# Inverting the 16x16 diagonal blocks of a delta-rule layer off TensorE: one block per partition on VectorE and GpSimd, carried through DRAM

## The chip, the cores and the metric

The kernel runs on one core of one Trainium2 chip. The metric is device time in microseconds (us) of one execution, the median of several. Before the change it is 2876.7 us, the median of three runs (2873.14, 2876.70 and 2880.99).

## What is computed

Two transformer layers on 4 sequences of 512 tokens with 256 features. Layer 0 adds to its input a gated delta-rule attention (32 value heads, 16 key heads, 128 features each) and a mixture of 64 experts; layer 1 adds a small attention and a mixture of 8 experts. The change touches the delta rule alone. The reference runs it token by token:

```python
def step(Sm, inp):
    q_, k_, v_, g_, b_ = inp
    Sm = Sm * jnp.exp(g_)[..., None, None]
    kv = jnp.einsum('bhk,bhkv->bhv', k_, Sm)
    delta = (v_ - kv) * b_[..., None]
    Sm = Sm + jnp.einsum('bhk,bhv->bhkv', k_, delta)
    o = jnp.einsum('bhk,bhkv->bhv', q_, Sm)
    return (Sm, o)
```

The kernel runs it in chunks of 128 tokens. Within a chunk the tokens depend on each other through a unit triangular 128x128 matrix, whose inverse is needed for every batch element and value head.

## The kernel before, in words

The program has three parts. The first (L65) normalizes the tokens, makes the gates and the routing. The second (`heads_and_experts`, L437) is the long one: 64 steps, one for each pair of key head and chunk (`STEPS`), each with 8 triangular matrices (2 value heads x 4 sequences). The third (L1774) gathers the experts' results and computes layer 1.

A step is written out by hand as a fixed order of calls for each engine, and three steps overlap: in step g the engines project and convolve step g's tokens, invert the matrices of step g-1, and use the inverses of step g-2. TensorE's order is in `step` at L945, ScalarE's (ACT) at L1236, VectorE's (DVE) at L1541, GpSimd's (POOL) at L1705 and that of the load queue (SP) at L690. Every engine works its list strictly in order, and semaphores join the lists; a call that waits holds everything behind it on its engine.

The matrix of step g is made by DVE in `decayed_products` (L1420, four multiplications of PSUM by the decays, tile `ATP`). ACT's `compact` (L1134) copies the 32x32 diagonal blocks into `ATc` (128 partitions x 256). These are inverted by doubling. `first_level` (L1430, DVE) makes the 2x2 inverses with a mask, a subtraction from the identity and a transpose. Then come four levels (1 to 4). Each is: 32 small products on TensorE (`level_x`, L789, two instruction records each), a copy on ACT (`inverse_copy`, L1151), 32 more products (`level_y`, L803), and on DVE `level` (L1441): a subtraction of PSUM and a 32x32 transpose. GpSimd makes the levels' masked operands in two calls of `mask` (L1639). Level 1 of a step begins late in that step, levels 2, 3 and 4 follow in the next. Levels 5 and 6 then join the 32x32 blocks to 64 and to 128.

Other calls that the text speaks of: `project` (L731) and `project_z` (L745), the projections of the tokens; `evacuate` (L1091, ACT), which copies a projection out of PSUM; `conv` (L1374, DVE), three multiply-adds for each of four channel groups, both tensor operands in SBUF; `squares` (L1119, ACT); `row_scales` (L1491, DVE), which waits for `out_squares` (L1200) and for `squares` of the queries, and runs a chain of small dependent operations (L50 to L58); `gather_out`, `residual`, `level6`, `outputs`, `new_state` and `rows_decay` on DVE; `scaled_decays`, `rho_w`, `gated`, `state_decay` and `normed` on GpSimd. In the first 8 steps GpSimd also issues 16 indirect DMAs per step (`scatter`, L1695). TensorE's `slot_free` (L714) makes a product wait until the PSUM bank that it reuses has been read: `project(g, 3)` waits there for the last of `decayed_products`, and the expert's gate product (`EX_GATE`, L939) for `squares` of the queries.

On SP each step loads, in this order, the decays of the step (`decays_in`, into the single tile `ab`), the step's expert (`unit_in`) and, for some steps, weights (`head_in`).

Of the kernel before, what the change touches and what calls it, by code (L numbers as in the profile page):

```python
# [5 lines left out]
F32 = mybir.dt.float32  # L6
# [58 lines left out]
def layernorm_and_gates(nc, A, R, adram, xnbuf, xbuf, routes):  # L65
# [7 lines left out]
    with ExitStack() as ctx:  # L73
# [59 lines left out]
        zero_set, zeroed = sem("zero_set"), sem("zeroed")  # L133
        head_loaded, head_high = sem("head_loaded"), sem("head_high")
        dve_step, pool_step = sem("dve_step"), sem("pool_step")
# [5 lines left out]
        def _(sp_):  # L141
# [8 lines left out]
            for dst, src in ((R["w_raw"][:, :, :], A["w_in"][0, :, :].rearrange("p (k n) -> p k n", k=KT)), (R["cw_raw"][:, :, :], A["conv_w"][0, :, :].rearrange("p (k n) -> p k n", k=4)),  # L150
                             (R["normw"][:, :], A["norm_w"]), (R["masks"][:, :, :], A["masks"]), (R["identc"][:, :], A["identc"])):
                sp_.dma_start(dst, src).then_inc(head_loaded, 16)
            sp_.wait_ge(zero_set, 1)
            for q in range(NE // 4):
                sp_.dma_start(xbuf[EARLY * CAP + q * 512:EARLY * CAP + (q + 1) * 512, :].rearrange("(p r) d -> p (r d)", p=P), zero[:, :]).then_inc(zeroed, 16)
# [9 lines left out]
            sp_.wait_ge(stored, 16 * (B + 3))  # L165
            sp_.wait_ge(zeroed, 16 * NE // 4)
# [89 lines left out]
        def _(dve):  # L256
# [36 lines left out]
            dve.wait_ge(head_loaded, 80)  # L293
# [68 lines left out]
            dve.tensor_tensor(put_u[:, :, :].bitcast(I32), slot_u[:, :, :].bitcast(I32), over_i[:, :, :], ALU.bitwise_or)  # L362

        @block.gpsimd
        def _(pool):
# [6 lines left out]
            pool.memset(zero[:, :], 0.0).then_inc(zero_set, 1)  # L372
# [19 lines left out]
            pool.memset(aT[:, :, :, 0:1], 0.0).then_inc(aT_copied, 1)  # L392

# [12 lines left out]
    inverse_mm=(("x2", 1), ("x6", 2), ("y6", 2), ("y2", 1), ("x3", 1), ("y3", 1), ("x4", 1), ("y4", 1), ("x5", 1), ("x1", 0), ("y1", 0), ("y5", 1)),  # L406
    inverse_sb=((6, 2), (2, 1), (3, 1), (4, 1), (1, 0), (5, 1)),
    inverse_d=((2, 1), (3, 1), (4, 1), (1, 0), (5, 1)),
# [5 lines left out]
LEVELS = 5  # L414
BLK = 32
PARTS = [(kt, wp, xp) for kt in range(KT) for wp, xp in ((0, 0), (0, 1), (1, 0))]
# [5 lines left out]
           compact=4, masked=2, halved=2, spread=4, t5=3, tt=1,  # L422
# [14 lines left out]
def heads_and_experts(nc, A, R, adram, xnbuf, xbuf, ybuf):  # L437
# [22 lines left out]
    with ExitStack() as ctx:  # L460
        sb = lambda n, s, d=F32: ctx.enter_context(nc.sbuf_tensor("p2_" + n, s, d))
        sem = lambda n: ctx.enter_context(nc.semaphore("p2_" + n))
        w_raw, w_hl, cw_raw, cw, masks, identc, normw = (R[n] for n in ("w_raw", "w_hl", "cw_raw", "cw", "masks", "identc", "normw"))
# [21 lines left out]
        M = sb("M", [P, LEVELS - 1, 2, B, BLK])  # L485
# [35 lines left out]
        dstep, init = sem("dstep"), sem("init")  # L521
# [77 lines left out]
        def vb(ap, n=BLK):  # L599
            return ap.rearrange("p (g t) -> p g t", t=n)  # L600

# [42 lines left out]
        def _(sp):  # L644
# [44 lines left out]

            def step(g):  # L690
                decays_in(g)
                unit_in(g)
                head_in(g)
# [3 lines left out]
            for j in range(TAIL):  # L697
                x_, gu_, d_ = tail_buffers(j)
# [14 lines left out]
        def _(pe):  # L713
# [75 lines left out]
            def level_x(g, l):  # L789
# [3 lines left out]
                wait(pe, "masked", g, 1 if l < 3 else 2)  # L793
                if l == 1:
                    wait(pe, "tt", g - 2, 1)
                pe.nop(nofuse=True)
                for n in range(2 * B):
                    v, b = n // B, n % B
                    for q in range(4):
                        m = pe.matmul(psI[p][quad(q), n * BLK:(n + 1) * BLK], M[quad(q), l - 1, v, b, :], Dc[p][quad(q), v, b, :], start=True, stop=True)  # L800
# [144 lines left out]
            def step(g):  # L945
                project(g, 0)
                if g >= 1:
                    level_x(g - 1, 2)
# [8 lines left out]
                if g >= 1:  # L957
                    level_y(g - 1, 2)
                if g >= 2:
# [5 lines left out]
                if g >= 1:  # L965
                    level_x(g - 1, 3)
                if g >= 2:
                    within(g - 2, 0)
                if g >= 1:
                    turn_values(g - 1, 0)  # L970
                    level_y(g - 1, 3)
# [24 lines left out]
                level_x(g, 1)  # L996
# [6 lines left out]
                level_y(g, 1)  # L1003
# [36 lines left out]
            level_x(STEPS - 1, 2)  # L1040
# [4 lines left out]
            level_y(STEPS - 1, 2)  # L1045
# [3 lines left out]
            level_x(STEPS - 1, 3)  # L1049
# [3 lines left out]
            level_y(STEPS - 1, 3)  # L1053
# [36 lines left out]
        def _(act):  # L1090
# [43 lines left out]
            def compact(g):  # L1134

                wait(act, "atp", g, 4)
                wait(act, "masked", g - 1, 2)
                wait_event(act, "inverse_d", 1, g - 1)
                for q in range(4):
                    act.activation(heads(ATc[quad(q), :, :, :]), heads(ATP[g % 2][quad(q), :, :, 0, quad(q)]), ACT.Copy).then_inc(s["compact"], 1)  # L1140
# [95 lines left out]
            def step(g):  # L1236
# [9 lines left out]
                if g >= 1:  # L1246
                    inverse_copy(g - 1, 2)
                if g >= 2:
# [11 lines left out]
                if g >= 1:  # L1260
                    inverse_copy(g - 1, 3)
                if g >= 2:
# [14 lines left out]
                compact(g)  # L1277
# [6 lines left out]
                inverse_copy(g, 1)  # L1284
# [34 lines left out]
            inverse_copy(STEPS - 1, 2)  # L1319
# [4 lines left out]
            inverse_copy(STEPS - 1, 3)  # L1324
# [36 lines left out]
        def _(dve):  # L1361
            count = [0]
# [67 lines left out]
            def first_level(g):  # L1430
# [972 lines left out]
```

## Time and profile before

| | |
|---|---|
| median of three runs | 2876.7 us |
| span of the profiled execution, first to last instruction | 2973.8 us |
| TensorE (PE) busy | 2684.9 us, 90% of the span |
| VectorE (DVE) busy | 2384.7 us, 80% |
| ScalarE (ACT) busy | 1828.3 us, 61% |
| GpSimd (POOL) busy | 1221.2 us, 41% |
| mean granted TensorE clock | 0.954 |

Times in the profile are microseconds unless marked ns. The profiled execution's own time is its span of 2973.8 us; no time beyond the span is listed for it, and it is 97.1 us longer than the median of the timed runs. In the page's slices of the span, PE is at nine tenths or more from about 300 us to 2500 us: the 64 steps. What lies before is the first part and the filling of the steps, what lies behind is their draining and layer 1. [...]

### The profile page before, as it was taken

The numbers are of one execution on the slowest core, as the hardware profiler recorded it, in microseconds if no ns is written. First come the engines' busy times: TensorE is split into PE (matmuls) and PEld (weight loads), VectorE is DVE, ScalarE is ACT, GpSimd is POOL, SyncE is SP. The second block draws the span as 40 slices with busy tenths as digits, with TensorE's granted clock in tenths as the row PEclk, the third lists the DMA queues.
The fourth block names the chain that finished last, engine by engine and source line by source line (L and its number), as shares of the span: only waits on it lengthen the run. The fifth ranks groups of instructions, "written<-read, shape, count | busy, mean of one in ns | idle before, by whom it ended". The sixth has DMA issues, their size and how long they took to land. (4 is left out here: it accounts for less than half of the span.)

```text
span 2973.8 us, 122804 instructions
## 1 busy us (share of the span) xinstructions
PE 2684.9 (90%) x52271; PEld 2275.1 (77%) x52272; DVE 2384.7 (80%) x5006; ACT 1828.3 (61%) x5749; POOL 1221.2 (41%) x1048
## 2 busy tenths in 40 slices
PE   1478889999999999999999999999999999857898
PEld 1367668888888888888888888888888888724555
DVE  7556658888888888888888888888888888468796
ACT  1245546777777777777777777777777777501111
POOL 2456555343434343434343434343434343255420
PEclk7778889999999999999999999999999999978999
DMA  5221101111111111111111111111111110152311
GB/s 189 92 61 42 32 23 38 35 42 35 42 35 42 35 42 35 42 36 41 39 42 41 39 39 42 41 40 37 42 35 42 35 32 28 61 192 90 94 64 43
DMA packets 92834, 153.27 MB, mean 52 GB/s; under 512 B 16966, under 2 KB 60661, under 8 KB 91107
## 3 DMA queue, kind: packets, MB, share of 16 engines
q1 hardware_dynamic: 69491, 111.65, 12.9%
q0 software_dynamic: 12288, 24.19, 2.6%
q10 hardware_dynamic: 10512, 9.57, 0.9%
q8 instruction: 415, 6.80, 0.9%
q14 instruction: 128, 1.05, 0.1%
HBM read 114.38 MB, written 40.37 MB: 52 GB/s over the span
## 5 line engine op out<-in xcount | busy, mean ns | idle before, releaser
L1383 DVE SCALAR_TENSOR_TENSOR p_y<-p_xr,cw,p_y 128x512 f32<-128x512 f32 x768 | 652.2, 851 | 66.7 <-ACT p_y L1101 46.6
L740 PE MATMUL p_psF<-xnS,w_hl 128*128 128x512 f32 x1536 | 432.8, 417 | 24.1 <-PEq L628 11.1
L1655 POOL TENSOR_TENSOR p_Wr<-p_Ws,p_rho 128x512 f32<-128x512 f32 x96 | 135.8, 1436 | 651.0 <-ACT p_Ws L1198 651.0
L740 PEld LDWEIGHTS p_psF<-xnS,w_hl 128*128 128x128 f32 x1536 | 279.3, 195 | 87.3 <-issue 18.2
L1637 POOL TENSOR_TENSOR p_E<-p_E,p_sj 128x512 f32<-128x512 f32 x128 | 158.0, 1253 | 292.9 <-DVE p_sj L1409 292.9
L800 PEld LDWEIGHTS p_psI<-p_Dc,p_M 32*32 32x32 f32 x16384 | 180.1, 106 | 100.0 <-issue 91.9
L922 PE MATMUL p_psO<-p_wout,p_ont 128*128 128x256 f32 x1024 | 250.4, 399 | 0.7 <-ACT p_ont L1211 0.7
L800 PE MATMUL p_psI<-p_Dc,p_M 32*32 32x32 f32 x16384 | 215.7, 195 | 38.1 <-issue 33.7
L1678 POOL TENSOR_TENSOR p_O<-p_OG,p_sm 128x512 f32<-128x512 f32 x128 | 131.4, 1049 | 240.9 <-DVE p_sm L58 240.8
L1098 ACT ACTIVATE p_xr<-p_psF 128x512 f32<-128x512 f32 x256 | 154.1, 602 | 123.0 <-PE p_psF L740 119.8
L810 PEld LDWEIGHTS p_psI<-p_Xs,p_DTc 32*32 32x32 f32 x16384 | 168.5, 106 | 75.0 <-issue 70.0
L810 PE MATMUL p_psI<-p_Xs,p_DTc 32*32 32x32 f32 x16384 | 199.3, 195 | 27.0 <-ACT p_Xs L1158 14.3
L922 PEld LDWEIGHTS p_psO<-p_wout,p_ont 128*128 128x128 f32 x1024 | 197.7, 198 | 30.2 <-ACT p_ont L1211 1.1
L1204 ACT ACTIVATE p_O<-p_OG 128x128 f32<-128x128 f32 x512 | 152.0, 298 | 111.4 <-POOL p_OG L1672 109.4
L755 PE MATMUL p_psF<-w_hl,xnS 128*128 128x256 f32 x1536 | 214.5, 290 | 5.0 <-issue 1.7
L755 PEld LDWEIGHTS p_psF<-w_hl,xnS 128*128 128x128 f32 x1536 | 198.8, 193 | 16.0 <-ACT p_y L1101 4.6
L1158 ACT ACTIVATE p_Xs<-p_psI 128x256 f32<-128x256 f32 x320 | 124.1, 388 | 126.0 <-PE p_psI L800 85.1
L1445 DVE TENSOR_TENSOR p_Dc<-p_Dc,p_psI 128x256 f32<-128x256 f32 x256 | 104.4, 408 | 97.6 <-PE p_psI L810 97.0
L1644 POOL TENSOR_TENSOR p_M<-p_ATc,masks 128x512 f32<-128x512 f32 x128 | 175.2, 1369 | 8.7 <-ACT p_ATc L1140 8.6
L1101 ACT ACTIVATE p_y<-p_psF,cw 128x512 f32<-128x512 f32 x256 | 176.8, 691 | 1.6
L1418 DVE TENSOR_TENSOR_SCAN p_E<-p_ab,p_identr 128x512 f32<-128x512 f32 x128 | 171.2, 1338 | 6.9 <-DMA p_ab<-decays 6.9
L1427 DVE TENSOR_TENSOR p_ATP<-p_psF,p_E 128x512 f32<-128x512 f32 x256 | 158.8, 681 | 22.4 <-PE p_psF L786 17.7
(322 smaller groups left out, 6638.8 us busy)
## 6 DMA issues: line engine op xcount, KB each, us to landing
p_ab<-decays SPq DMA_DIRECT2D x64, 512.0 KB
w_raw<-in_w_in SPq DMA_DIRECT2D x16, 768.0 KB, 5.6
p_wgu<-in_w_gu SPq DMA_DIRECT2D x60, 176.0 KB
expert_out<-p_ye ACTq DMA_DIRECT2D x73, 128.0 KB, 1.8
expert_in<-p_zero SPq DMA_DIRECT2D x16, 512.0 KB, 7.1
p_xe<-expert_in SPq DMA_DIRECT2D x60, 128.0 KB
p_wd<-in_w_down SPq DMA_DIRECT2D x60, 88.0 KB
p_wout<-in_w_out SPq DMA_DIRECT2D x16, 256.0 KB
```

The lines of the kernel that those rows point to most:

```text
L740: m = pe.matmul(b4(psF[f % 2][:, :]), w_hl[:, wp, kt, ty * P:(ty + 1) * P], xnS[:, xp, kt, :].rearrange("p (b t) -> p b t", b=B)[:, :, c * ...
L755: m = pe.matmul(psF[f % 2][:, (b % 2) * 2 * P:(b % 2 + 1) * 2 * P], xnS[:, xp, kt, b * S + c * P:b * S + (c + 1) * P], w_hl[:, wp, kt, 4 * ...
L800: m = pe.matmul(psI[p][quad(q), n * BLK:(n + 1) * BLK], M[quad(q), l - 1, v, b, :], Dc[p][quad(q), v, b, :], start=True, stop=True)
L810: m = pe.matmul(psI[p][quad(q), 256 + n * BLK:256 + (n + 1) * BLK], DTc[p][quad(q), v, b, :], Xs[p][quad(q), v, b, :], start=True, stop=True)
L922: m = pe.matmul(psOO[:, b * D:(b + 1) * D], ont[:, v, b, :], wout[:, v, :], start=(v == 0), stop=(v == 1))
L1098: act.activation(xr[:, ty, :, TAPS - 1:], b4(psF[f % 2][:, :]), ACT.Copy)
L1101: act.activation(y[:, ty, :, :], b4(psF[f % 2][:, :]), ACT.Copy, scale=cw[:, ty, TAPS - 1:TAPS]).then_inc(s["drained"], 1)
L1383: m = dve.scalar_tensor_tensor(y[:, ty, :, :], xr[:, ty, :, tap:tap + P], cw[:, ty, tap:tap + 1], y[:, ty, :, :], ALU.mult, ALU.add)
L1418: dve.tensor_tensor_scan(flat(E[:, v, :, :]), flat(ab[:, v, :, :]), flat(identr[:, :, :]), 0.0, ALU.mult, ALU.add).then_inc(s["scan"], 1)
L1427: dve.tensor_tensor(ATP[g % 2][:, v, two, :, :], psF[f % 2][:, :].rearrange("p (b u t) -> p b u t", b=2, u=2), E[:, v, two, :].unsqueeze(2 ...
L1637: pool.tensor_tensor(E[:, v, :, :], E[:, v, :, :], over(sj[:, :, v]), ALU.mult).then_inc(s["diag"], 1)
L1644: pool.tensor_tensor(M[:, two, :, :, :].rearrange("p l v b t -> p l (v b) t"), heads(ATc[:, :, :, :]).unsqueeze(1).to_broadcast([P, 2, 2 * ...
```

## The change

The 32x32 blocks are no longer built up from 2x2. Each holds two 16x16 blocks on its diagonal, 64 of them in a step; these are inverted one per partition, and only level 4 (16 to 32) stays on TensorE. Per step:

- ACT: `compact(g)` writes the negated blocks and moves forward in its list, ahead of `squares(g, 1)`. The copies of levels 1 to 3 are gone.
- SP: `cores_out(g)` stores `ATc` to a DRAM buffer, waits, and loads the 64 blocks into `U`, one per partition, by two DMAs of 512 runs of 64 bytes. `cores_back(g-1)` waits for the inverses, stores them by two such DMAs into a second DRAM buffer (whose other elements stay zero), waits, and loads that buffer into `DTc`. A step's order is now `cores_back(g-1)`, the loads of step g+1, `cores_out(g)`, the weights of step g+1.
- DVE: `pivots(g-1)` at the place of `level(g-1, 1)`: a memset of the diagonals, then for k = 1 to 6 a product and an addition on both 8x8 halves of 64 partitions (12 to 24 elements per partition), each waiting for the one before. `turn_cores(g-1)`, one 32x32 transpose, at the place of `level(g-1, 3)`; it waits for the load into `DTc`. `first_level` and levels 1, 2 and 3 are gone.
- GpSimd: `join(g-1)` at the head of its step: two 8x8 matrix products per partition, each a multiplication of 512 elements and additions of 256, 128 and 64, all in a chain. The two calls of `mask` become one of half the size.
- TensorE: `level_x` and `level_y` of levels 1, 2 and 3 are gone: 192 small products per step.

```diff
+            def cores_out(g):
+                wait(sp, "compact", g, 4)
+                sp.dma_start(block_rows(blocks_out), ATc[:, :, :, :].rearrange("p v b t -> p (v b t)")).then_inc(apart, 16)
+                sp.wait_ge(apart, 16 * (g + 1))
+                for s_ in range(2):
+                    at = slice(s_ * CORES // 2, (s_ + 1) * CORES // 2)
+                    sp.dma_start(U[at, 0:CORE * CORE], core_rows(blocks_out, s_)).then_inc(gathered, 16)
+
+            def cores_back(g):
...
+                wait(sp, "joined", g, 1)
+                for s_ in range(2):
+                    at = slice(s_ * CORES // 2, (s_ + 1) * CORES // 2)
+                    sp.dma_start(core_rows(blocks_back, s_), U[at, 0:CORE * CORE]).then_inc(returned, 16)
+                sp.wait_ge(returned, 16 + 32 * (g + 1))
+                wait(sp, "spread", g - 2, 4)
+                sp.dma_start(DTc[g % 2][:, :, :, :].rearrange("p v b t -> p (v b t)"), block_rows(blocks_back)).then_inc(inverted, 16)
...
             def step(g):
-                decays_in(g)
-                unit_in(g)
-                head_in(g)
+                cores_back(g - 1)
+                loads(g + 1)
+                cores_out(g)
+                if g + 1 < STEPS:
+                    head_in(g + 1)
...
-            def first_level(g):
+            def pivots(g):
+
+                dve.wait_ge(gathered, 32 * (g + 1))
+                mark(dve.memset(diagonal, 1.0))
+                for k in range(1, HALF_CORE - 1):
+                    n = HALF_CORE - 1 - k
+                    column = halves_of[:, :, 0:k, k:k + 1].to_broadcast([CORES, 2, k, n])
+                    row = halves_of[:, :, k:k + 1, k + 1:].to_broadcast([CORES, 2, k, n])
+                    rest, product = halves_of[:, :, 0:k, k + 1:], pivot[:, :, 0:k, 0:n]
+                    link(dve.tensor_tensor(product, column, row, ALU.mult))
+                    m = dve.tensor_tensor(rest, rest, product, ALU.add)
+                    if k < HALF_CORE - 2:
+                        link(m)
+                m.then_inc(s["pivoted"], 1)
+
+            def turn_cores(g):
 
                 p = g % 2
                 wait(dve, "halved", g - 2, 2)
-                wait(dve, "spread", g - 2, 4)
                 wait_event(dve, "inverse_mm", "x5", g - 2)
-                wait(dve, "compact", g, 4)
-                link(dve.tensor_tensor(heads(Dc[p][:, :, :, :]), heads(ATc[:, :, :, :]), masks[:, 0, :].unsqueeze(1).to_broadcast([P, 2 * B, BLK]), ALU.mult))
-                link(dve.tensor_tensor(heads(DTc[p][:, :, :, :]), identc[:, :].unsqueeze(1).to_broadcast([P, 2 * B, BLK]), heads(Dc[p][:, :, :, :]), ALU.subtract))
+                dve.wait_ge(inverted, 16 * (g + 1))
                 dve.transpose(heads(Dc[p][:, :, :, :]), heads(DTc[p][:, :, :, :])).then_inc(s["inverse_d"], 1)
...
+            def join(g):
+
+                n = [CORES, HALF_CORE, HALF_CORE, HALF_CORE]
+                lo, hi = slice(0, HALF_CORE), slice(HALF_CORE, CORE)
+                wait(pool, "pivoted", g, 1)
+                for half, left, right in ((0, square[:, lo, lo], square[:, lo, hi]), (1, halfway[:, :, :], square[:, hi, hi])):
+                    link(pool.tensor_tensor(terms[:, :, :, :], left.rearrange("p i k -> p k i").unsqueeze(3).to_broadcast(n), right.unsqueeze(2).to_broadcast(n), ALU.mult))
+                    for k in (4, 2):
+                        link(pool.tensor_tensor(terms[:, 0:k, :, :], terms[:, 0:k, :, :], terms[:, k:2 * k, :, :], ALU.add))
+                    if half == 0:
+                        link(pool.tensor_tensor(halfway[:, :, :], terms[:, 0, :, :], terms[:, 1, :, :], ALU.add))
+                    else:
+                        pool.tensor_tensor(square[:, lo, hi], terms[:, 0, :, :], terms[:, 1, :, :], ALU.add).then_inc(s["joined"], 1)
...
                 if g >= 2:
                     out_squares(g - 2, 0)
                     out_squares(g - 2, 1)
+                compact(g)
                 squares(g, 1)
                 if g >= 1:
                     inverse_copy(g - 1, 4)
                 evacuate(g, 3)
                 expert(g, EX_GATE)
-                compact(g)
```

## Rows read from the trace of the kernel before

**Rows 1.** Windows: busy us of each engine (x instructions), granted clock, DMA share, GB/s.
```profile
800.00:1600.00 800.00, 783.37 (x17483) 692.36 (x17482) 687.13 (x1358) 595.59 (x1913) 316.74 (x264) 1.00 0.15 39
282.00:340.00 58.00, 46.70 (x815) 38.85 (x812) 35.07 (x66) 27.19 (x88) 39.81 (x37) 0.82 0.13 43
```

**Rows 2.** One line's instructions: DVE's gather_out, once a step (ns min/median/max, first and last start).
```profile
L1514 DVE TENSOR_TENSOR acc<-acc,p_psO x43: 1181/1182/1184, 812.7 to 2356.7; 128x1024 f32<-128x1024 f32 x43
```

**Rows 3.** Timeline, TensorE, one step: start, us, what [idle before].
```profile
1530.65 0.60 PE L939 MATMUL p_psF<-p_xeT,p_wgu 128*88 128x128 f32 x4
...
1547.98 0.75 PE L800 MATMUL p_psI<-p_Dc,p_M 32*32 32x32 f32 x64
1548.67 1.14 PE L846 MATMUL p_psI<-p_D64X,p_ATP 64*64 64x64 f32 x16
```

**Rows 4.** Timeline, VectorE, the same step.
```profile
1525.49 2.48 DVE L1427 TENSOR_TENSOR p_ATP<-p_psF,p_E 128x512 f32<-128x512 f32 x4 [0.39 <-PE p_psF L786]
...
1530.36 0.17 DVE L1502 TENSOR_SCALAR p_xq<-p_ss 128x4 f32<-128x4 f32 x1 [0.46 <-ACT p_y L1126]
...
1534.52 0.74 DVE L1437 TENSOR_TENSOR p_Dc<-p_ATc,masks 128x256 f32<-128x256 f32 x1
1535.29 1.41 DVE L1438 TENSOR_TENSOR p_DTc<-identc,p_Dc 128x256 f32<-128x256 f32 x1
...
1537.89 3.58 DVE L1383 SCALAR_TENSOR_TENSOR p_y<-p_xr,cw,p_y 128x512 f32<-128x512 f32 x3
...
1545.95 0.42 DVE L1445 TENSOR_TENSOR p_Dc<-p_Dc,p_psI 128x256 f32<-128x256 f32 x1 [0.43 <-PE p_psI L810]
1546.41 0.45 DVE L1446 STREAM_TRANSPOSE p_DTc<-p_Dc 128x256 f32<-128x256 f32 x1
1546.78 1.18 DVE L1514 TENSOR_TENSOR acc<-acc,p_psO 128x1024 f32<-128x1024 f32 x1
...
1549.42 2.33 DVE L1383 SCALAR_TENSOR_TENSOR p_y<-p_xr,cw,p_y 128x512 f32<-128x512 f32 x3 [0.43 <-ACT p_y L1101]
...
1553.84 0.68 DVE L1450 TENSOR_SCALAR p_TT<-p_psI 64x512 f32<-64x512 f32 x1 [1.05 <-PE p_psI L855]
...
1560.73 0.42 DVE L1445 TENSOR_TENSOR p_Dc<-p_Dc,p_psI 128x256 f32<-128x256 f32 x1 [0.44 <-PE p_psI L810]
...
1562.90 2.48 DVE L1427 TENSOR_TENSOR p_ATP<-p_psF,p_E 128x512 f32<-128x512 f32 x4 [0.39 <-PE p_psF L786]
```

**Rows 5.** Groups by line, 800 to 2400 us: busy us, mean ns | idle before.
```profile
L56 DVE TENSOR_TENSOR p_sm<-p_sm 128x12 f32<-128x12 f32 x129 | 22.1, 171 | 4.4
```

**Rows 6.** Timeline, ACT, the same step: the four copies of compact.
```profile
1531.61 1.72 ACT L1140 ACTIVATE p_ATc<-p_ATP 32x256 f32<-32x256 f32 x4
```

**Rows 7.** Timeline, GpSimd: first part, then the same step.
```profile
61.33 2.17 POOL L385 TENSOR_TENSOR p_sp<-p_sp,p_pl 128x512 f32<-128x512 f32 x1 [11.96 <-DVE p_pl L320]
...
1538.88 1.26 POOL L1644 TENSOR_TENSOR p_M<-p_ATc,masks 128x512 f32<-128x512 f32 x1
```

**Rows 8.** One line's instructions: GpSimd's smallest product, 800 to 2400 us.
```profile
L1686 POOL TENSOR_TENSOR p_hb<-p_gsb,p_usb x44: 451/682/909, 804.1 to 2389.2; 88x128 f32<-88x128 f32 x44
```

**Rows 9.** DMA issues: count, KB each, median us from issue to landing.
```profile
expert_out<-p_ye ACTq DMA_DIRECT2D x73, 128.0 KB, 1.8
...
p_wbc<-expert_weights SPq DMA_DIRECT2D x4, 512.0 KB, 5.1
```

**Rows 10.** Timeline, the load queue, the same step.
```profile
1559.37 0.39 SPq L648 DMA_DIRECT2D p_ab<-decays  x1
```

**Rows 11.** Timeline, TensorE: a wait ahead of a half-speed stretch.
```profile
469.68 0.60 PE L821 MATMUL p_psI<-p_Dc,p_ATP 32*32 32x32 f32 x27 [1.22 <-DVE p_DTc L1446]
```

**Rows 12.** Windows around it: columns as in rows 1.
```profile
460.00:471.20 11.20, 8.70 (x200) 6.67 (x199) 10.58 (x25) 5.31 (x11) 8.71 (x9) 1.00 0.03 6
471.20:474.60 3.40, 3.40 (x9) 2.78 (x9) 3.36 (x5) 3.13 (x8) 2.27 (x2) 0.50 0.00 0
```

More of the change, by code:

```diff
@@ L164, in _ @@
             sp_.dma_start(routes[:, 2 * NT * NE:], kept[:, 2 * NT * NE:]).then_inc(stored, 16)
-            sp_.wait_ge(stored, 16 * (B + 3))
-            sp_.wait_ge(zeroed, 16 * NE // 4)
+            sp_.wait_ge(stored, 16 * (B + 3 + NE // 4))
         @block.tensor
@@ L370, in link @@
                 ch.wait()
-            pool.memset(zero[:, :], 0.0).then_inc(zero_set, 1)
+            ch.then(pool.memset(zero[:, :], 0.0))
             pool.wait_ge(consts_loaded, 16 * n_consts)
@@ L520, in heads_and_experts @@
         w_in, w_high, w_split, cw_in, wo_in, wo_ready = (sem(n) for n in ("w_in", "w_high", "w_split", "cw_in", "wo_in", "wo_ready"))
-        dstep, init = sem("dstep"), sem("init")
+        init = sem("init")
+        apart, gathered, returned, inverted = (sem(n) for n in ("apart", "gathered", "returned", "inverted"))
         def wait(eng, name, g, n):
@@ L697, in _ @@
             for j in range(TAIL):
+                if j == TAIL_BUFS:
+                    cores_back(STEPS - 1)
                 x_, gu_, d_ = tail_buffers(j)
@@ L792, in level_x @@
                 wait_event(pe, "inverse_d", l, g)
-                wait(pe, "masked", g, 1 if l < 3 else 2)
-                if l == 1:
-                    wait(pe, "tt", g - 2, 1)
+                wait(pe, "masked", g, 1)
+                wait(pe, "tt", g - 2, 1)
                 pe.nop(nofuse=True)
@@ L1136, in compact @@
                 wait(act, "atp", g, 4)
-                wait(act, "masked", g - 1, 2)
-                wait_event(act, "inverse_d", 1, g - 1)
+                wait(act, "masked", g - 1, 1)
+                if g:
+                    act.wait_ge(apart, 16 * g)
                 for q in range(4):
-                    act.activation(heads(ATc[quad(q), :, :, :]), heads(ATP[g % 2][quad(q), :, :, 0, quad(q)]), ACT.Copy).then_inc(s["compact"], 1)
+                    act.activation(heads(ATc[quad(q), :, :, :]), heads(ATP[g % 2][quad(q), :, :, 0, quad(q)]), ACT.Copy, scale=-1.0).then_inc(s["compact"], 1)
             def values(g, v):
@@ L1545, in step @@
                 if g >= 1:
-                    level(g - 1, 1)
+                    pivots(g - 1)
                 if g >= 3:
@@ L1555, in step @@
                 if g >= 1:
-                    level(g - 1, 2)
                     history(g - 1, 1)
@@ L1563, in step @@
                 if g >= 1:
-                    level(g - 1, 3)
+                    turn_cores(g - 1)
                 if g >= 2:
@@ L1573, in step @@
                     new_state(g - 2, 0)
-                first_level(g)
                 if g >= 1:
@@ L1595, in _ @@
             history(STEPS - 1, 0)
-            level(STEPS - 1, 1)
+            pivots(STEPS - 1)
             gather_out(STEPS - 3)
@@ L1600, in _ @@
             level6(STEPS - 2)
-            level(STEPS - 1, 2)
             history(STEPS - 1, 1)
             outputs(STEPS - 2, 0)
-            level(STEPS - 1, 3)
+            turn_cores(STEPS - 1)
             outputs(STEPS - 2, 1)
@@ L1628, in _ @@
             gather_out(STEPS - 1)
+            R["dve_steps"] = count[0]
         @block.gpsimd
@@ L1705, in step @@
             def step(g):
+                if g >= 1:
+                    join(g - 1)
                 scatter(g, 0)
@@ L1708, in step @@
                 scatter(g, 2)
-                if g >= 1:
-                    mask(g - 1, 1)
                 scatter(g, 3)
@@ L1728, in step @@
                     normed(g - 2)
-                mask(g, 0)
+                mask(g)
                 scatter(g, 11)
@@ L1740, in _ @@
                 step(g)
-            mask(STEPS - 1, 1)
+            join(STEPS - 1)
             rho_w(STEPS - 2)
@@ L2357, in constants @@
     f, p, j, g = np.float32, np.arange(P), np.arange(BLK), np.arange(NG)
-    joins = [(j[:, None] // (2 * n) == j // (2 * n)) & (j[:, None] % (2 * n) < n) & (j % (2 * n) >= n) for n in (1, 2, 4, 8, 16)]
+    join = (j[:, None] < CORE) & (j >= CORE)
     inv = (1.0 / 10000.0 ** (np.arange(0, DH1, 2, dtype=f) / f(DH1))).astype(f)
```

110 lines of the change are left out of this document (58 added, 52 removed).

## The prediction, made before the change was run

> **What bounds the kernel now.** I read the windows first. Between 800 and 1600 us TensorE is busy 783 of 800 us at full clock, VectorE 687, ScalarE 596, GpSimd 317 [rows 1]. So in the steady steps TensorE is the bound, and VectorE is close behind. `gather_out` runs once a step: 43 starts from 812.7 to 2356.7 us make 42 steps of 36.8 us [rows 2]. Then I read one typical step on each engine's timeline. From the start of `decayed_products` at 1525.49 to the next at 1562.90 it is 37.4 us [rows 4]. There TensorE hardly pauses, while VectorE has short waits for TensorE (0.43, 1.05 and 0.44 us) and for ACT (0.46, 0.43) [rows 4]. The changed kernel takes work from both, so the question is which chain of waits replaces TensorE's work as the bound.
>
> **TensorE.** One removed group of small products holds TensorE for 0.69 us (1547.98 to 1548.67) [rows 3]. Six such groups go, 4.1 us a step. If nothing else came late a step would be 37.4 - 4.1 = 33.3 us. That is the lower bound.
>
> **VectorE, ACT and the mask.** Removed on VectorE: two operations of `first_level`, 0.74 + 1.41 = 2.15 us, and three levels of 0.42 + 0.45 = 0.87 us [rows 4]; `first_level`'s transpose stays, at another place. Added: 12 dependent small operations. The newton chain, of the same kind with 12 elements, takes 171 ns each with 4.4 us idle over 129, 0.205 us apart [rows 5]; with the memset `pivots` is 2.6 us. Three copies of ACT go too; they cost nothing now, since ACT is busy 596 of 800 us. One removed call of `mask` ran 1.26 us on GpSimd beside a convolution, which took 3.58 us there against 2.33 us elsewhere [rows 4, 7].
>
> **Contention that comes.** `join` now starts on GpSimd when `pivots` ends, and runs beside `conv(g, 0)`. The same two rows price this: a GpSimd operation of 1.26 us made three convolution operations 1.25 us longer. I take 1.3 us; bounds 0 (no overlap) and 3.8 (each of the three waits for one such operation). [...]
>
> **The moved compact.** `compact` takes 1.72 us on ACT [rows 6] and now stands ahead of `squares(g, 1)`. Behind `squares` wait VectorE's `row_scales` and TensorE's `EX_GATE`. VectorE's operation that needs it began 2.39 us after `decayed_products` had ended (1527.97 to 1530.36) and waited for ACT [rows 4], so it moves to 4.1 us. `EX_GATE` began 2.68 us after that end (1530.65) [rows 3], without a wait; it becomes 4.1 us too. That is a new wait of 1.4 us on TensorE in each step, with all of TensorE's second half queued behind it.
>
> **The loop that I expect to bind.** It goes from the end of `decayed_products` over ACT to TensorE, and back by ACT to VectorE.
> - End of `decayed_products` to `EX_GATE`: 4.1 us.
> - `EX_GATE` to the next `conv(g, 0)`: 1549.42 - 1530.65 = 18.8 us before [rows 3, 4], less level 1's two groups (1.4 us): 17.4 us.
> - `conv(g, 0)` to the end of `decayed_products`: 1565.38 - 1549.42 = 16.0 us before [rows 4]. Levels 2 and 3 go (1.74), the waits for TensorE of 1.05 and 0.44 go, as its products come earlier; `turn_cores` adds 0.45 and contention 1.3: 14.5 us.
>
> The sum is 36.0 us, against 37.4: a gain of 1.4 us a step. VectorE alone has some 0.9 us to spare ahead of `conv(g, 0)`: 21.45 us from 1527.97 to 1549.42, plus 1.72, less 2.15, 0.87, two waits of 0.43 and the 1.26 of contention that goes, plus 2.6, is 20.6 us, against 4.1 + 17.4 = 21.5.
>
> **The new chain over DRAM.** Two stretches must fit. The outward one (`compact`, store, loads) has half a step and costs nothing. The inward one has from the end of `pivots` to `turn_cores`. In it VectorE has `gather_out` and `residual` (1546.78 to 1549.42 less 0.43: 2.2 us), the spare 0.9, and `conv(g, 0)` to the place of level 3 (1560.73 - 1549.42 = 11.3, less 0.87, 1.05 and 0.44, plus 1.3: 10.25) [rows 4]: 13.4 us. It must hold `join` and two hops through DRAM.
> - `join`: GpSimd took 1.26 us for 512 elements [rows 7] and at best 0.451 us for 128 [rows 8], so about 2.1 ns an element; 256 is 0.72, 64 is 0.31 us. Two chains of 1.26 + 0.72 + 0.45 + 0.31 make 5.5 us, and 1.3 us for its own waits on the convolution. Upper bound: the slow row of 2.17 us for 512 [rows 7], 1.7 times as much, 9.4 us.
> - The hops: landing took 1.8 us for 128 KB stored and 5.1 us for a large load [rows 9]. Both hops are 128 KB or less, so I take near the lower, 2.5 us each and 0.4 for the second issue [rows 10]: 5.4 us, bounds 4.0 and 10.6.
>
> Together 12.2 us within 13.4: `turn_cores` waits for nothing, with 1.2 us left. This is thin. The packets of 64 bytes have no like row. [...]
>
> **SP.** The next decays and expert are now queued behind `cores_back(g-1)`, and `head_in` behind `cores_out`. The decays' load was issued at 1559.37 [rows 10], 12.6 us after the step's `gather_out` (1546.78) [rows 4], and its tile is first read in the next step, over 20 us later; `cores_back` ends at about the same place. Zero; the cover is that slack, and if it were gone the scan at the step's start would wait.
>
> **First eight steps and the drain.** Here GpSimd issues the scatters; it is busy 39.8 of 58 us and TensorE's clock is 0.82 [rows 1]. `join` holds back scatters that formerly ran ahead, while the levels' round trips go. I take zero, bounds -1.4 and +6 us a step. In the drain three round trips are exchanged for one long one: zero.
>
> **Sum.** 56 steps x 1.4 us = 78 us of the profiled span of 2973.8, 2.6%. The span is 3.4% longer than the median run (2876.7), so I carry the share over: 2876.7 x (1 - 78/2973.8) = 2801 us.
>
> **Rivals.**
> 1. *TensorE stays the bound.* The waits close up and contention falls between operations: 33.3 us a step, 56 x 4.1 = 230 us, 2654 us. For it: TensorE's 783 of 800 us. Against: the 1.4 us that `compact` puts into the loop.
> 2. *The inward chain comes late* (slower). Place: VectorE waits in `turn_cores`, with `decayed_products` and then TensorE behind it. With `join` at 9.4 us and the hops midway between their bounds, 7.3 us, the chain is 16.7 us, the wait 3.3, the step 39.3: 56 x 1.9 = 106 us more, 2980 us. It decides from a chain of 13.4 + 1.4 = 14.8 us on. For it: no like row for 8x8 operands on GpSimd or 64-byte packets. Against: rows 8 and 9.
> [...]
>
> **How the numbers follow.** Forecast 0.43, rival 1 0.18, rival 2 0.16, rival 3 0.17, and 0.06 for a sum that happens to cancel. The forecast's own range, with contention 0 to 3.8, is 2730 to 2937 (34.7 to 38.5 us a step). The range 2670 to 2980 leaves out rival 1 at its full price and rival 2 with longer hops. A measurement of this kernel can tell 0.3%, 9 us, from no change. Faster 0.60, same 0.08, slower 0.32: rivals 2 and 3 are slower, and rival 3 and the upper end of the forecast share the middle.
>
> **What would show it.** Right: the steady step is 35 to 36.5 us; TensorE's small products of L800 and L810 are a quarter in number; TensorE waits about 1.4 us for `squares` ahead of `EX_GATE`; `pivots` takes 2.6 us; `turn_cores` is ready when VectorE comes to it; the granted clock stays 1.0. [...] The forecast is wrong if the step is below 34 or above 37.4 us.

## The result, and the profile after

The changed kernel is slower by 0.7%: 2899.2 us, the median of 4 runs, against 2878.6 us for 4 runs of the kernel before beside it; ratio 1.0071, 95% interval 1.0056 to 1.0086. The forecast was 2801 us.

The page of the profile after (span; busy time, share of the span and instructions of each engine), against the table above:

```profile
span 2898.0 us, 74166 instructions
...
PE 2479.0 (86%) x27696; PEld 2063.7 (71%) x27696; DVE 2237.3 (77%) x5326; ACT 1761.6 (61%) x5557; POOL 1521.1 (52%) x1496
```

Against the execution shown above, TensorE has lost half of its instructions and 206 us of busy time, VectorE 147 us; GpSimd has gained 300 us. In the steady steps TensorE was busy 783 of 800 us [rows 1]. The windows view (the same columns as [rows 1]) and the group of `gather_out` between 800 and 2400 us after, which answer to [rows 1] and [rows 2]:

```profile
800.00:1600.00 800.00, 727.27 (x9090) 629.40 (x9089) 638.96 (x1476) 572.72 (x1854) 425.81 (x422) 0.97 0.20 49
```
```profile
L1556 DVE TENSOR_TENSOR acc<-acc,p_psO x44: 1204/1206/1209, 801.5 to 2377.6; 128x1024 f32<-128x1024 f32 x44
```

43 steps in 1576.1 us are 36.65 us each, against 36.8 [rows 2]. TensorE now idles 73 us of 800, and the steps are hardly shorter: the work that was taken away has been replaced by waits. The waits of VectorE and TensorE in the same stretch of the kernel after (engine, line, waited for: us in total, times, longest):

```profile
DVE p_xq L1544 <- ACT p_y L1164: 113.6, 44, 2.8
DVE p_Dc L1481 <- DMA p_DTc<-blocks_back: 58.5, 29, 3.9
```
```profile
PE p_psF L992 <- ACT p_y L1164: 56.5, 38, 2.3
PE p_psI L853 <- DVE p_Dc L1481: 31.5, 18, 3.1
```

The first and the third row are `row_scales` and `EX_GATE` behind `squares`, which `compact` now precedes; the second is `turn_cores` waiting for the blocks from DRAM; the fourth is level 4's first product behind `turn_cores`, so this wait reaches TensorE.

**A trap in the spans.** Against the span of 2973.8 us shown for before, 2898.0 us would be a gain of 76 us, almost the 78 us of the forecast. Only the times say otherwise. That is why the first experiment ran the kernel before again.

### The profile page after: what moved, and what is told of

Read it like the earlier page. It is cut to its first block and busy times, and to the rows that moved or that the text cites. A ratio compares the mean times of both kernels' runs of the same rounds, so it can differ in the third digit from the quotient of the medians.

```text
span 2898.0 us, 74166 instructions
## 1 busy us (share of the span) xinstructions
PE 2479.0 (86%) x27696; PEld 2063.7 (71%) x27696; DVE 2237.3 (77%) x5326; ACT 1761.6 (61%) x5557; POOL 1521.1 (52%) x1496
## 5 line engine op out<-in xcount | busy, mean ns | idle before, releaser
L809 PE MATMUL p_psF<-w_hl,xnS 128*128 128x256 f32 x1536 | 230.6, 304 | 2.2 <-ACT p_y L1139 2.2
L809 PEld LDWEIGHTS p_psF<-w_hl,xnS 128*128 128x128 f32 x1536 | 214.7, 208 | 13.9 <-ACT p_y L1139 3.3
L1698 POOL TENSOR_TENSOR p_terms<-p_U 64x512 f32<-64x512 f32 x64 | 74.2, 1159 | 279.2 <-DVE p_U L1470 279.2
L1700 POOL TENSOR_TENSOR p_terms<-p_terms 64x256 f32<-64x256 f32 (+1 forms) x256 | 200.0, 781 | 20.1
L1731 POOL TENSOR_TENSOR p_OG<-p_O,p_zs 128x512 f32<-128x512 f32 x128 | 160.6, 1267 | 56.5 <-DVE p_O L1512 46.1
L1714 POOL TENSOR_TENSOR p_Wr<-p_Ws,p_rho 128x512 f32<-128x512 f32 x96 | 124.0, 1313 | 90.6 <-ACT p_Ws L1237 89.3
L949 PE MATMUL p_psO<-p_Ws,p_ATP 128*128 128x128 f32 x1024 | 143.6, 283 | 25.9 <-ACT p_O L1230 23.0
L1155 ACT ACTIVATE p_zs<-p_psF 128x512 f32<-128x512 f32 x128 | 75.9, 593 | 129.9 <-PE p_psF L809 129.9
L949 PEld LDWEIGHTS p_psO<-p_Ws,p_ATP 128*128 128x128 f32 x1024 | 124.0, 191 | 40.7 <-issue 37.9
L1187 ACT ACTIVATE p_vs<-p_psF,p_vsc 128x128 f32<-128x128 f32 x512 | 148.1, 395 | 4.0 <-PE p_psF L818 4.0
```

The source lines that it names most:

```text
L809: m = pe.matmul(psF[f % 2][:, (b % 2) * 2 * P:(b % 2 + 1) * 2 * P], xnS[:, xp, kt, b * S + c * P:b * S + (c + 1) * P], w_hl[:, wp, kt, 4 * ...
L949: m = pe.matmul(psO[v][:, b * P:(b + 1) * P], ATP[g % 2][:, v, b, 1, :], Ws[:, v, b, :], start=True, stop=True)
L1700: link(pool.tensor_tensor(terms[:, 0:k, :, :], terms[:, 0:k, :, :], terms[:, k:2 * k, :, :], ALU.add))
L1731: pool.tensor_tensor(OG[:, v, :, :], O1[:, v, :, :], zs[g % 2][:, v, :, :], ALU.mult).then_inc(s["og"], 1)
```

## The experiments

### The kernel before, once more

> The kernel before, unchanged. What it decides: whether the profiled span of 2973.8 us is the kernel's own time or a stretched one, since its timed runs stand at 2873 to 2881 us. Theory A (the profiled execution of before is longer than its unprofiled ones; the share of 2.6% was therefore taken from a span that overstated TensorE's small products): timed median 2870 to 2890 us, and its profiled execution again 2960 to 2985 us with gather_out every 36.8 us. Theory B (that one execution was long by chance; the change's additions ate what the removal gave): the profiled execution now agrees with the timed ones, a span of 2870 to 2890 us and gather_out every 35.2 to 35.6 us.

2875.4 us, ratio 1.0001 (0.9990 to 1.0012). Its profiled execution now spans 2876.2 us. The windows of both profiled executions of before, cut at the first `gather_out`, five steps later, and 56 steps after that; first the execution shown ahead, then the new one (us, busy time of PE, PEld, DVE, ACT and POOL with instructions, clock, DMA share, GB/s):

```profile
0.00:240.90 240.90, 119.69 (x1781) 95.23 (x1783) 145.94 (x327) 73.19 (x202) 103.97 (x93) 0.76 0.32 108
240.90:480.50 239.60, 205.57 (x3954) 173.36 (x3953) 165.15 (x321) 131.35 (x423) 149.03 (x132) 0.88 0.11 31
480.50:2541.50 2061.00, 2012.27 (x44788) 1779.85 (x44786) 1763.03 (x3510) 1530.43 (x4924) 818.27 (x684) 1.00 0.14 39
```
```profile
0.00:208.20 208.20, 105.67 (x1781) 86.37 (x1783) 145.80 (x326) 73.33 (x202) 100.06 (x89) 0.81 0.36 124
208.20:408.40 200.20, 185.59 (x3954) 161.78 (x3953) 167.30 (x320) 131.50 (x422) 155.03 (x137) 0.95 0.14 39
408.40:2469.70 2061.30, 2012.36 (x44788) 1779.82 (x44786) 1762.11 (x3511) 1528.51 (x4925) 818.22 (x684) 1.00 0.14 39
```

The 56 steady steps are the same, 2061 us. The 97.6 us lie outside them: 32.7 before the first `gather_out`, 39.4 in the next five steps, 26 behind the last. So theory A falls, TensorE's small products are not stretched, and theory B holds in that the long span did not come again, but not in the 35.2 to 35.6 us that it gave for a step: the steady step is 36.8 us. What delayed those parts was not tried. Now the two kernels can be compared part by part, by starts of `gather_out`:

| us | before, run again | after | difference |
|---|---|---|---|
| start to the first `gather_out` | 208.2 | 216.7 | +8.5 |
| the next 5 steps | 200.2 | 219.1 | +18.9 |
| the next 56 steps | 2061.3 | 2047.7 | -13.6 |
| the last 2 steps | 65.2 | 70.2 | +5.0 |
| from there to the end | 341.3 | 344.4 | +3.1 |

Two questions follow: why 56 steps gained 13.6 us and not 78, and why the first ones lost 27.

### What the removal is worth

```diff
 level_x, level_y
-                for n in range(2 * B):
+                for n in range(0 if l == 4 or g < 2 else 2 * B - 1, 2 * B):
```

> The kernel before, but in the steps from the third on the products of levels 1 to 3 are issued for one of the 8 heads alone, 4 of 32 in each of the six groups; all waits, copies and VectorE's operations stay. The other heads' inverses are left out of the computation. What it decides: what TensorE's small products of these levels are worth by themselves. By the row of 0.69 us a group, 7/8 of six groups are 3.6 us a step, 230 us over the steps. Theory B (the price was right): 2640 to 2720 us, less only as far as waits on VectorE or ACT take their place. Theory A (the price in the profile is too high by some 1.5 us a step, 95 us over 64 steps): 2720 to 2790 us. Rival C (TensorE was never the only bound, and the waits of the three round trips, which all stay, take its place): above 2800 us.

2757.7 us, ratio 0.9596 (0.9580 to 0.9612), 34.9 us a step. The products were priced at 3.6 us a step. Over the 56 steady steps TensorE's busy time fell by 2.6 us a step (from 35.9 to 33.3) and the step by 1.9. The number lies in the range of theory A, and in part its reason holds: 1.0 us of the price was not in the busy time. The other 0.7 us went into waits, as rival C has it, though not to the extent that it expected.

Then the levels as a whole (the calls of levels 1 to 3 taken from TensorE's, ACT's and VectorE's lists; `inverse_d` starts at level 4):

> The kernel before without levels 1 to 3: their products, ACT's copies and VectorE's subtractions and transposes go; first_level, both masks and the place of compact stay. That leaves the three doublings out of the computation. It is the removal without the additions. Theory (by the thinned kernel, which gained 117 us with all round trips in place, and VectorE's 2.6 us a step that go too): 33.3 to 34.0 us a step, 155 to 195 us less, 2680 to 2720 us. Rival (VectorE or the loop over ACT binds at once, the round trips had cost nothing): 2740 to 2770 us as the thinned one.

2743.3 us, ratio 0.9529 (0.9514 to 0.9545), 34.7 us a step. This is the rival. With work priced at 4.1 us on TensorE and 2.6 us on VectorE gone from each step, TensorE's busy time is 3.1 us less and the step 2.1 us shorter. The lower bound of 33.3 us is not reached.

### What the place of compact costs

The changed kernel with `compact` back at its old place, then the kernel before with `compact` at the new one:

```diff
 ACT, step
-                compact(g)
                 squares(g, 1)
...
                 expert(g, EX_GATE)
+                compact(g)
```

> The changed kernel with compact back behind EX_GATE's activation in ACT's list, as before. My theory of the loop (decayed_products, ACT, EX_GATE, conv 0): the wait of EX_GATE for squares (1.3 to 1.5 us a step) goes and the step falls by 1.0 to 1.4 us: 56 steps, 56 to 78 us less, 2820 to 2843 us, ratio 0.98 to 0.988 of before. Rival (another chain binds, the one over join and DRAM with turn_cores, or VectorE's own work): the outward hop starts 1.5 to 3 us later with half a step of room, the time stays at 2890 to 2905 us, and turn_cores' wait is as long as it was or longer.

2792.9 us, ratio 0.9701 (0.9685 to 0.9717): 106 us less than the changed kernel, more than the theory gave. The rival falls, though the outward hop starts later.

> The kernel before with nothing but compact moved ahead of squares, the place that it has in the changed kernel. Theory (the move by itself delays EX_GATE and row_scales in a loop without slack): 1.4 to 1.9 us a step, 80 to 106 us, 2955 to 2981 us. Rival (the wait costs only where TensorE has become short of work; before, the levels' products fill it): less than 30 us, 2875 to 2905 us.

2984.2 us, ratio 1.0359 (1.0334 to 1.0383): 107 us more than before. The move has the same price in either kernel, 107 and 106 us (1.9 and 1.7 us in each of the 56 steps), so TensorE's small products did not cover it. TensorE's timeline in this kernel, the end of the products that `decayed_products` reads and `EX_GATE`:

```profile
1507.87 1.89 PE L786 MATMUL p_psF<-p_kq 128*128 128x256 f32 x8
...
1515.62 0.67 PE L939 MATMUL p_psF<-p_xeT,p_wgu 128*88 128x128 f32 x4 [1.38 <-ACT p_y L1126]
```

`EX_GATE` had no wait before [rows 3]. Over the steady steps, the end of `decayed_products` to `EX_GATE` is 2.33 us in the kernel before, 3.96 in this one (+1.63), 3.91 in the changed kernel and 2.55 with `compact` back.

### What join costs, and where

```diff
-                wait(sp, "joined", g, 1)
+                wait(sp, "pivoted", g, 1)
...
-                    join(g - 1)
```

> The changed kernel without join on GpSimd: the stores of the inverted blocks wait for pivots alone. The upper right 8x8 parts stay as they came, which leaves that part of the inverse out of the computation. Theory: join costs the step in two ways, as contention with conv 0 (0.9 to 1.1 us) and as turn_cores' wait for DRAM (1.35 us a step on the average); the chain is 7 us shorter, both go, and the step falls by 1.5 to 2.3 us: 84 to 130 us less, 2770 to 2815 us. Rival (the loop over compact and EX_GATE binds, what VectorE saves it waits for again): less than 30 us gained, 2870 to 2905 us.

2806.8 us, ratio 0.9766 (0.9746 to 0.9786): 92 us less. 16.4 us of it lie before the first `gather_out` and 31.3 in the next five steps; the 56 steps give 42. Then `join` run, but off the chain (its last addition writes to a tile that nothing reads; the next `cores_out` waits for it, so that its operands are not overwritten):

> The changed kernel with join still run on GpSimd, but its result put into a tile that nothing reads, and the stores waiting for pivots alone (the upper right 8x8 parts of the inverse are left out): join's work stays, its place in the chain over DRAM goes. Without join at all it was 92 us less, 47 of it up to the ninth gather_out and 42 in the steady steps. Theory (in the first steps it is GpSimd's time that costs, in the steady ones the chain, seen as turn_cores' wait of 1.35 us a step): the early 47 us stay lost, the steady steps fall by 0.6 to 0.75 us: 35 to 45 us less, 2855 to 2865 us. Rival (contention with conv 0 is the steady loss too): nothing gained, 2890 to 2905 us.

2876.3 us, ratio 1.0003 (0.9993 to 1.0012): 23 us less, between the two theories. The first steps are as long as with `join` (217.5 and 219.2 us), so there it is GpSimd's time that costs. The steady steps fall by 0.32 us of the 0.75 that `join` costs them. This is a net figure: no `turn_cores` waits any more, and by the kinds of step of the table below the head change and the third fall by 2.7 and 0.9 us. But in the first and the second `EX_GATE` now waits 2.3 and 2.2 us for `squares`, not 1.2 and 0.6, and they rise by 1.4 and 1.0 us. The other 0.43 go with `join`'s work on GpSimd. `conv(g, 0)`, which runs beside it, took 3.03 us on the average in the changed kernel, 2.99 here, and 2.32 without `join`; what the calls of GpSimd behind `join` add was not tried apart.

Both edits together:

> The changed kernel with compact back behind EX_GATE's activation and also without join (the upper right 8x8 parts of the inverse are left out). By themselves the two edits gave 106 and 92 us. Theory (two separate losses, one in the loop of compact and EX_GATE, one on GpSimd and in the chain over DRAM): together 180 to 200 us, 2700 to 2720 us. Rival (they draw on one slack, or VectorE is the bound in either case): 2750 us or more.

2698.7 us, ratio 0.9381 (0.9365 to 0.9398). 200 us less than the changed kernel, 106 + 92 = 198 by the single edits: two separate losses, and the rival falls.

### The first steps

```diff
 VectorE, step: behind pivots(g - 1)
+                    if g <= SPREAD_STEPS:
+                        join_early(g - 1)
 GpSimd, step
-                if g >= 1:
+                if g > SPREAD_STEPS:
                     join(g - 1)
```

> The changed kernel with compact back behind EX_GATE's activation, and with join on VectorE, behind pivots, in the first nine steps alone, in which GpSimd issues the scatters; from then on join is on GpSimd as before. Theory (in these steps GpSimd is the bound and join holds back the scatters; without join they were 47 us shorter): VectorE's join takes about 3 us there and is covered in part, 25 to 45 us less than the 2793 us with compact late: 2748 to 2768 us. Rival (VectorE's own operations wait as long as GpSimd's did): 2785 to 2800 us.

2759.3 us, ratio 0.9594 (0.9574 to 0.9614): 34 us less than with `compact` late alone. To the sixth `gather_out` it takes 404.7 us instead of 432.1. With this, `join`'s time on GpSimd, where it stands in front of the scatters, is shown as the loss of the first steps.

### One step in four

The cycle from the end of one `decayed_products` to the end of the next, split as in the prediction's loop; means of 11 cycles each, over 44 steady steps, from the starts and ends on the timelines, before to after. A head has four steps, and each row is the cycle from one of them into the next: "first" from the third step into the fourth, "head change" from the fourth into the next head's first, where the next weights are split, "second" from the first into the second, "third" from the second into the third.

| us | to `EX_GATE` | to `conv` 0 | to `decayed_products` | itself | cycle before | cycle after |
|---|---|---|---|---|---|---|
| first | 2.5 to 3.8 | 19.1 to 17.6 | 13.6 to 11.8 | 2.5 | 37.6 | 35.7 |
| head change | 2.7 to 4.7 | 19.6 to 20.2 | 13.1 to 14.1 | 2.5 | 37.8 | 41.4 |
| second | 2.7 to 3.7 | 18.8 to 17.4 | 13.6 to 11.8 | 2.5 | 37.6 | 35.4 |
| third | 1.6 to 3.4 | 17.5 to 15.7 | 12.8 to 12.5 | 2.5 | 34.3 | 34.1 |

Three of the four gained 1.4 us on the average (1.9, 2.2, 0.2). The fourth, the head change, lost 3.6 us: over 14 heads 50 us, against 60 that the other 42 cycles gained. It lost in every leg: 2.0 us up to `EX_GATE` (the others 1.0 to 1.8), 0.6 from there to `conv` 0, where the others became 1.4 to 1.8 shorter, and 1.0 behind it, where the first and second became 1.8 shorter. `turn_cores` waited 2.7 us on the average in the head change, 2.4 in the third, which is why that one gained only 0.2 (33.0 us with `join` off the chain), 0.2 in the second and nothing in the first. The head change's timeline on VectorE, GpSimd and SP in the kernel after:

```profile
1585.08 2.46 DVE L1457 TENSOR_TENSOR p_ATP<-p_psF,p_E 128x512 f32<-128x512 f32 x4
...
1603.98 0.76 DVE L574 CAST w_hl<-w_raw 128x512 fp32r<-128x512 f32 x2
1604.69 2.26 DVE L1448 TENSOR_TENSOR_SCAN p_E<-p_ab,p_identr 128x512 f32<-128x512 f32 x1
...
1606.90 1.14 DVE L1469 TENSOR_TENSOR p_pivot<-p_U 64x12 f32<-64x12 f32 x1
...
1610.24 1.21 DVE L1556 TENSOR_TENSOR acc<-acc,p_psO 128x1024 f32<-128x1024 f32 x1
...
1626.86 0.45 DVE L1481 STREAM_TRANSPOSE p_Dc<-p_DTc 128x256 f32<-128x256 f32 x1 [3.92 <-DMA p_DTc<-blocks_back]
...
1627.81 2.47 DVE L1457 TENSOR_TENSOR p_ATP<-p_psF,p_E 128x512 f32<-128x512 f32 x4
```
```profile
1604.49 3.53 POOL L578 TENSOR_TENSOR w_hl<-w_raw,w_hl 128x512 fp32r<-128x512 f32 x2 [2.18 <-DVE w_hl L574]
...
1618.05 0.65 POOL L1704 TENSOR_TENSOR p_U<-p_terms 64x64 f32<-64x64 f32 x1
```
```profile
1623.02 0.56 SPq L730 DMA_DIRECT2D p_DTc<-blocks_back  x1
```

Here VectorE casts the next weights, and GpSimd splits them beside the scan (2.26 us here; the step's other scan, 16 us later, took 1.21) and the first product of `pivots` (1.14 us against 0.14 to 0.17). `gather_out` starts 25.2 us after `decayed_products`; in the kernel before it was 22.6 us in such a step. `join` ends at 1618.7, the blocks are back at 1626.8, and `turn_cores` has waited 3.9 us. The same edit in both kernels tests it: only 8 of each 256 columns are split.

```diff
-            dve.tensor_copy(w_hl[:, 0, :, 2 * n * P:2 * (n + 1) * P], ...)
+            dve.tensor_copy(w_hl[:, 0, :, 2 * n * P:2 * n * P + 8], ...)
```

> The kernel before, with the splitting of the next head's weights into two parts (VectorE's next_weights and GpSimd's) done for 8 of each 256 columns; the rest of the next weights is left out of the computation. It is the base for the same edit of the changed kernel. In every fourth step VectorE spends 1.2 us and GpSimd 4.8 us on it. Expected by each theory: that step falls from 37.8 us to the 37.5 of its neighbours or less, 14 steps by 0.3 to 2 us: 5 to 30 us less, 2845 to 2870 us.

2888.2 us, ratio 1.0043 (1.0028 to 1.0059): a miss, 12 us more instead of less. The head-change cycle is 39.0 us, with the longer leg behind `conv(g, 0)`. That mean is made of two kinds. Seven of the eleven cycles take 37.4 to 38.5 us. In the other four TensorE stands for 1.1 to 2.7 us, some 23 us after `decayed_products`, waiting for nothing that the profile shows; a half-speed stretch (granted clock 0.50) goes with it, and they take 40.2 to 42.9 us. What stops TensorE there is open.

> The changed kernel with the same edit. Between before and after the cycle from decayed_products to decayed_products went from 37.6 to 35.7, 37.6 to 35.4 and 34.3 to 34.1 us in three steps of four, 1.4 us less on the average, and from 37.8 to 41.4 in the fourth, where the next head's weights are split. Theory (the splitting, on VectorE ahead of pivots and on GpSimd ahead of join, starts the chain over DRAM late in that step, and so eats what the others gained): with it short that step falls by 3 to 5 us, 42 to 70 us less in 14 steps, 2830 to 2857 us, at or below the kernel before with the same edit. Rival (the load of the next head's 768 KB of weights on the same queue lengthens the two hops, 8.2 us against 6.0; the splitting does not matter): less than 25 us, 2875 us or more.

2846.2 us, ratio 0.9897 (0.9881 to 0.9912): 53 us less, as the theory said. The head-change cycle falls from 41.4 to 37.5 us, and the changed kernel is now faster than before with the same edit, 2846.2 / 2888.2 = 0.985, and than before without it, 0.990. The second cycle gives a part back, 37.2 us instead of 35.4: in nine of eleven a half-speed stretch now follows `EX_GATE` (37.4 to 37.6 us; 36.1 and 36.4 in the two without). Over the 56 steps the step is 35.8 us, 1.0 less than before, where it was 0.2 less with the split. `turn_cores` in such a step of this kernel has no wait (VectorE's timeline):

```profile
1551.83 2.46 DVE L1457 TENSOR_TENSOR p_ATP<-p_psF,p_E 128x512 f32<-128x512 f32 x4
...
1587.24 0.43 DVE L1481 STREAM_TRANSPOSE p_Dc<-p_DTc 128x256 f32<-128x256 f32 x1
...
1589.24 2.48 DVE L1457 TENSOR_TENSOR p_ATP<-p_psF,p_E 128x512 f32<-128x512 f32 x4 [0.77 <-PE p_psF L840]
```

`gather_out` starts 21.8 us after `decayed_products`, not 25.2. The other explanation, the load of the next weights on SP's queue, was tried on the kernel of 2759 us:

```diff
-                if c == 0 and kh + 1 < HK:
+                if c == 1 and kh + 1 < HK:
 SP, step
                 loads(g + 1)
+                next_head_in(g + 1)
                 cores_out(g)
```

> The kernel with compact late and VectorE's join in the first nine steps (2759 us), and in addition SP issues the load of the next head's weights one step later and ahead of cores_out instead of behind it, away from join's hops. Theory (that load lengthens the hops by 2.2 us in the head's first step, and turn_cores waits for it): up to 2.2 us in each of 14 steps, 15 to 31 us less, 2728 to 2744 us. Rival (the splitting alone makes the chain late): 2750 to 2765 us.

2758.8 us, ratio 0.9594 (0.9575 to 0.9612): nothing gained, and the head-change cycle stays (38.7 against 38.6 us). That load is not the cause. Nor does it help to let `gather_out` go ahead of `pivots` in that step:

> The kernel with compact late and VectorE's join in the first steps, and in addition gather_out ahead of pivots in each head's first step (15 of the steady steps). There TensorE waited 2.3 us for gather_out. Theory (that wait is the bound there): 1.0 to 2.3 us in each such step, 15 to 35 us less than 2759: 2725 to 2745 us. Rival (the chain of join starts 1.2 us later, and turn_cores waits for it instead): 2750 to 2775 us.

2757.2 us, ratio 0.9588 (0.9574 to 0.9602). The step between `gather_out` in question fell from 38.8 to 35.4 us, and the next one rose from 34.1 to 37.7: the chain starts later and gives it back, as the rival said.

### The clock

```diff
 TensorE, state_update
-                for b in range(B):
+                for b in list(range(B)) * (1 + v):
```

> The changed kernel with one more group of products on TensorE ahead of EX_GATE: state_update of the second half is issued twice, 1.05 us a step of work with no use. Theory of the clock (the wait at EX_GATE is followed by stretches at half clock, 28 of them, 96 us in all, between 480 and 2400 us): TensorE is busy through the wait, most stretches go, and the time falls by 20 to 50 us, 2850 to 2880 us, though there is more work. Rival (the stretches lie in slack, and the wait is set by ACT): the added group hides in the wait, 2890 to 2910 us; if TensorE is the bound ahead of EX_GATE, 1.05 us a step more, up to 2960 us.

2888.0 us, ratio 1.0055 (1.0040 to 1.0071): 11 us less, with 0.9 us more work in each step (the two groups together take 1.95 us, the one took 1.05). Between 480 and 2400 us the record of the granted clock has 15 half-speed stretches, 65 us, instead of 28 and 96 us. The windows of this kernel, against 0.97 in the changed one:

```profile
800.00:1600.00 800.00, 738.52 (x9279) 640.27 (x9269) 639.88 (x1482) 577.96 (x1866) 425.60 (x425) 0.99 0.20 49
```

The theory holds in kind; 2888.0 lies just above its 2850 to 2880, so the clock is a small part of the loss. It is not what makes the head change long, though 21 of the 28 stretches of the changed kernel lie there. Two of its eleven cycles have full clock until their last 3 us and still take 41.6 and 41.8 us; the first of them up to there:

```profile
1148.10:1186.90 38.80, 32.09 (x367) 27.83 (x368) 30.56 (x69) 26.81 (x89) 24.98 (x23) 1.00 0.21 56
```

What a stretch costs shows in the first kind of cycle of the changed kernel. In the three with a stretch right behind `EX_GATE`, the leg from there to `conv` 0 takes 18.5 to 18.6 us, in the others 17.25: 1.3 us.

## Why the prediction was wrong

- **TensorE, 0.69 us a group, six groups.** Too high, and as a gain about twice too high. With products priced at 3.6 us gone the busy time fell by 2.6 and the step by 1.9; with the levels gone (4.1 priced) by 3.1 and 2.1. The waits for ACT and VectorE behind them close up only in part. Rival 1 is out: TensorE is idle for 73 of 800 us.
- **VectorE.** `pivots` took 2.4 us (2.6 forecast), and 3.4 beside GpSimd's split.
- **Contention.** 0.7 us in `conv(g, 0)` (3.03 against 2.32), not 1.3. That lies within the bounds of 0 to 3.8 us. In the head change a product of `pivots` of 0.14 us took 1.14 beside GpSimd's split.
- **The moved compact.** Seen, placed and nearly sized: `EX_GATE` at 3.91 us after the end of `decayed_products` (4.1 forecast), with a wait of 1.3 us a step on the average (1.4 forecast). By itself, in the kernel before, the move costs 1.9 us a step, 107 us; the sum gave it 1.4.
- **The loop.** 4.1 + 17.4 + 14.5 = 36.0 us stands for three of the four steps: 35.7, 35.4 and 34.1 us, a mean gain of 1.43 against the 1.4 forecast. That the mean agrees so well is partly luck, since the single gains are 1.9, 2.2 and 0.2 and several terms missed both ways.
- **The step that failed is "56 steps x 1.4 us".** The typical step stood for all, and in it "`turn_cores` waits for nothing". The rows had a sign of more than one kind: 36.8 us on the mean [rows 2], 37.4 in the step that was read. In the head change the weights are split on VectorE ahead of `pivots` and on GpSimd ahead of `join`; the forecast left both out, though `next_weights` stands there in both kernels. There the cycle became 3.6 us longer instead of 1.4 shorter, and `turn_cores` waited 2.7 us. With the split short the cycle is 37.5 us, and 44 of the 64 us missing in the steady steps come back.
- **The chain over DRAM.** Where `turn_cores` waited for it, 14.4 us from `pivots` to `turn_cores` (15.4 in the head change), not 12.2, with room for 13.4: 7.7 for `join` (6.8 forecast), 2.6 from the issue of the stores to that of the load and 4.1 from there to the transpose (5.4 forecast for the two). Rival 2's mechanism is real, in 29 of 44 steps, above all in the head change and the third; its price of 106 us is not, since taking `join` off the chain gives 23. The hops were 1.3 us above the estimate; what part the runs of 64 bytes have in that is open, since they have this length in every kernel here that has them.
- **"First eight steps: I take zero."** The second failure: +27 us by the sixth `gather_out`, inside the bounds given (6 us a step), and shown to be `join`'s time on GpSimd, in front of the scatters. The drain, also taken as zero, cost 8 us.
- **Rival 3: TensorE's clock falls (chance 0.17).** Before, a wait of 1.22 us was followed by 3.4 us at half clock [rows 11, 12]; half of that, 1.7 us, can be estimated as the price of one such stretch. The clock did fall, to 0.97 between 800 and 1600 us, with 28 half-speed stretches between 480 and 2400 us; one costs 1.3 us where it falls in the binding loop, but there is not one in each step. Filling TensorE's wait took 13 of them away and gave 11 us.
- **The span.** Carrying the share over to the median did little harm (2 us), but the execution that was read had 72 us more than the same kernel run again, in the start and the first steps, where the forecast took zero.

Forecast for the steady steps -78, found -13.6; forecast for the rest 0, found +35.5 (8.5 + 18.9 + 5.0 + 3.1). The sum is +21.9 us, against 20.6 measured.

The kernel that beats both is the change with `compact` behind `EX_GATE` and the early `join` on VectorE: 2759 us, 4.1% below before. With only `compact` put back the change gains 82 us over before (2792.9 against 2875.2); the move of that one call costs 106.

## What to carry to other kernels

Split the steady state into its kinds of step before a typical one is multiplied; the step with extra work, here one in four, is where a longer chain comes late first. An operation that waits for a late event, put in an in-order list ahead of operations that do not need it, delays all of them (it cost 107 us in the kernel before and 106 in the changed one): try its place by itself, in both kernels. And hold the profiled span against the times; where they differ, profile the old kernel again before two spans are compared.

## What was not expected of the hardware

Two profiled executions of one program differed by 97.6 us while 56 of its steps agreed within 0.3 us in 2061; the clock granted in the long parts was lower (0.88 against 0.95 in the five steps after the first `gather_out`). And 0.9 us of useless TensorE work a step made the changed kernel 11 us faster, with 15 half-speed stretches (granted clock 0.50) between 480 and 2400 us instead of 28.
